# Head blocks of the memory update: eight narrow matmuls against two full ones with a mask

## The reference, cut to what matters

```
log_D = where(tril, cs[t] - cs[s], -inf) + ig[s];  D_mat = exp(log_D - max_log_D)
C = (q @ k.T / sqrt(32)) * D_mat                       # per head, 512 x 512
normalizer = max(|C.sum(-1)|, exp(-max_log_D))
h = (C / (normalizer + EPS)) @ v                       # then a layer norm over all heads
x = x + tanh(g_xattn) * h
```

## Time and profile before

| what | value |
| --- | --- |
| median of 3 runs | 799.27 us (798.9 to 800.16) |
| the profiled execution | 800.16 us, of which the span from first to last instruction is 798.2 us |
| busy, share of the span | PE 84%, DVE 64%, POOL 52%, ACT 47% |
| mean granted TensorE clock | 0.816 of 2.4 GHz |

### The profile page before, as it was taken

The page is one execution under the profiler, slowest core; times in us unless marked ns, Lnnn a source line. Parts: engine busy times, 40 slices in busy tenths (PEclk is TensorE's granted clock), DMA queues, the critical chain, the costliest instruction groups (busy, mean ns, idle before and its releaser), DMA issues.

```text
span 798.2 us, 18309 instructions
## 1 busy us (share of the span) xinstructions
PE 674.4 (84%) x6306; PEld 534.4 (67%) x6306; DVE 514.0 (64%) x1371; ACT 375.3 (47%) x941; POOL 411.3 (52%) x369
## 2 busy tenths in 40 slices
PE   2973879988998795067999999999999999999993
PEld 1531435554656564046998988989989889889893
DVE  7727787878877787973555564655555655555561
ACT  4335556766677754063444443443444443434441
POOL 5025499998998883012254444353444544534523
PEclk9995555555556655559999999999999999999998
DMA  9722878987988922173498897897988978969752
GB/s 285 263 94 61 246 249 270 292 244 255 302 273 271 290 105 67 14 303 122 133 276 271 241 286 232 236 307 217 272 261 261 273 245 236 309 206 287 252 147 50
DMA packets 85819, 179.74 MB, mean 225 GB/s; under 512 B 14881, under 2 KB 48546, under 8 KB 85730
## 3 DMA queue, kind: packets, MB, share of 16 engines
q1 hardware_dynamic: 63202, 140.10, 54.5%
q0 software_dynamic: 13824, 18.43, 10.9%
q10 hardware_dynamic: 8704, 20.06, 6.6%
HBM read 140.93 MB, written 38.67 MB: 225 GB/s over the span
## 4 chain that ended last, share of the span: by engine, by line
PE 51%; POOL 19%; DVE 11%; issue 9%; DMA 7%; ACT 2%; POOLq 0%; DVEq 0%; ACTq 0%
PE bank L1075 41%; POOL whl L469 8%; DMA out<-res,TS 4%; POOL x L699 3%; POOL vp L547 2%; DMA xg<-y_d,TG 2%; POOL qE L563 2%; PE bank L298 2%; PE bank L301 2%; PE bank L1069 2%; POOL kw L555 1%; POOL vp L545 1%; DMA w_d<-whl 1%; DVE R L970 1%; PE bank L510 1%
## 5 line engine op out<-in xcount | busy, mean ns | idle before, releaser
L1075 PE MATMUL bank<-xh,w 128*128 128x256 bf16 (+1 forms) x1760 | 268.2, 263 | 9.9 <-DVE xl L1131 8.2
L1057 POOL DMA_INDIRECT out<-res,TS x72 | 115.8, 1609 | 217.2 <-DMA out<-res,TS 97.8
L1075 PE MATMUL bank<-xl,w 128*128 128x256 bf16 (+1 forms) x880 | 222.5, 263 | 0.0
L1148 ACT ACTIVATE sg<-bank 128x256 f32<-128x256 f32 (+1 forms) x240 | 86.8, 362 | 232.2 <-PE bank L1075 220.1
L1075 PEld LDWEIGHTS bank<-xh,w 128*128 128x128 bf16 x1760 | 165.7, 98 | 28.5 <-issue 12.0
L1178 DVE TENSOR_TENSOR hf<-sg,bank 128x256 f32<-128x256 f32 (+1 forms) x200 | 78.9, 395 | 121.3 <-ACT sg L1148 114.7
L1075 PE MATMUL bank<-w,hh 128*128 128x256 bf16 x864 | 140.0, 273 | 0.0
L1048 POOL DMA_INDIRECT xg<-y_d,TG x72 | 72.5, 1006 | 79.0 <-DVE TS L1005 48.4
L469 POOL TENSOR_TENSOR whl<-wst,whl 128x1224 bf16<-128x1224 f32 x32 | 80.1, 2507 | 44.0 <-ACT whl L457 44.0
L1075 PE MATMUL bank<-w,hlo 128*128 128x256 bf16 x360 | 98.1, 273 | 0.0
L1142 ACT CAST hh<-hf 128x256 bf16<-128x256 f32 (+1 forms) x240 | 90.4, 377 | 12.6 <-DVE hf L1180 11.0
(11 more groups left out here) (218 smaller groups left out, 1079.9 us busy)
## 6 DMA issues: line engine op xcount, KB each, us to landing
w<-w_d SPq DMA_DIRECT2D x40, 1408.0 KB
w<-w_d SPq DMA_DIRECT2D x40, 768.0 KB
wst<-in_wts SPq DMA_DIRECT2D x32, 612.0 KB, 4.5
w_d<-whl ACTq DMA_DIRECT2D x32, 612.0 KB, 6.1
vb<-in_kv SPq DMA_DIRECT2D x8, 528.0 KB, 5.9
xa<-in_x SPq DMA_DIRECT2D x8, 512.0 KB, 8.3
kT<-in_kv SPq DMA_DIRECT2D x8, 512.0 KB, 8.8
xc<-in_x SPq DMA_DIRECT2D x8, 512.0 KB, 6.0
```

What stands on the lines that cost most here:

```text
L1057: nc.gpsimd.indirect_dma_start(out, bass.IndirectOffsetOnAxis(ap=TS[:, c0:c0 + 1], axis=0), res[w][:, j, :], None, bounds_check=TOK - 1, o ...
L1075: mm = nc.tensor.matmul(dst, l, r, start=(n == 0), stop=(n == len(pairs) - 1))
L1148: nc.scalar.activation(sg[m % 2][0:K, 0:N], bank[0:K, 2 + (NM * w + m) % 4, 0:N], ACT.Silu).then_inc(f_sg, 1)
```

## The change

The state update is computed as two full matmuls, all four heads of a group against all four; the blocks off the diagonal are then multiplied by zero on DVE, in the same operation that applies the scale 1/sqrt(32). For chunks 1 and 2 the masked product goes into a new SBUF tile `Ut`, and the update of the state reads `Ut` in place of PSUM. The mask `blkm` is made at the start, from one more index table on POOL and three more operations on DVE; the one clearing of PSUM goes away.

```diff
@@ consts_pool
+            nc.gpsimd.iota(blk[:, :].rearrange("p (h e) -> p h e", e=DV), [[DH, HG], [0, DV]], base=0,
+                           channel_multiplier=0, allow_small_or_imprecise_dtypes=True).then_inc(s_iota, 1)
@@ consts_dve
-            dve.wait_ge(s_iota, 4)
+            dve.wait_ge(s_iota, 5)
...
-
-            dve.wait_ge(s_const, 9)
+            nc.vector.tensor_scalar(blkt[:, :], blk[:, :], float(DH), pcol[:, 0:1], ALU.add, ALU.is_gt).then_inc(s_const, 1)
+            nc.vector.tensor_scalar(blkm[:, :], blk[:, :], pcol[:, 0:1], None, ALU.is_le).then_inc(s_const, 1)
+            dve.wait_ge(s_const, 11)
+            nc.vector.tensor_tensor(blkm[:, :], blkm[:, :], blkt[:, :], ALU.mult).then_inc(s_const, 1)
+
@@ g_actf_all
-                    nc.scalar.activation(dst, src, ACT.Copy, scale=SCALE).then_inc(g_cols, 1)
+                    nc.scalar.copy(dst, src).then_inc(g_cols, 1)
@@ g_pe_all, g_dvef
-            pe.wait_ge(b_uz, 1)
...
-            V.memset(bank[:, 4:6, UO:UO + HG * DV], 0.0).then_inc(b_uz, 1)
@@ b_s_pe
-                    for j in range(HG):
-                        hd = g * HG + j
-                        mm = nc.tensor.matmul(bank[DH * j:DH * (j + 1), 4 + g, UO + DV * j:UO + DV * (j + 1)],
-                                              kw[u % 2][:, DH * hd:DH * (hd + 1)], vv(u)[:, DV * hd:DV * (hd + 1)],
-                                              start=True, stop=True)
+                    mm = nc.tensor.matmul(bank[:, 4 + g, UO:UO + HG * DV], kw[u % 2][:, g * P:(g + 1) * P],
+                                          vv(u)[:, g * HG * DV:(g + 1) * HG * DV], start=True, stop=True)
@@ b_st_dve
-                ge(dve, b_h, t)
+                mask = blkm[:, :].unsqueeze(1).to_broadcast([P, 2, HG * DV])
                 if c == 0:
-                    V.tensor_copy(St[0][:, :, :], ub).then_inc(b_st, 1)
+                    ge(dve, b_h, t)
+                    V.scalar_tensor_tensor(St[0][:, :, :], ub, SCALE, mask, ALU.mult, ALU.mult).then_inc(b_st, 1)
                 else:
+                    V.scalar_tensor_tensor(Ut[:, :, :], ub, SCALE, mask, ALU.mult, ALU.mult).then_inc(b_ut, 1)
                     if t == 1:
                         ge(dve, s_dec, 16 * HG)
+                    ge(dve, b_ut, b * 2 + c)
+                    ge(dve, b_h, t)
                     for g in range(2):
                         ins = V.scalar_tensor_tensor(St[c % 2][:, g, :], St[1 - c % 2][:, g, :], dec[:, b, g, c:c + 1],
-                                                     ub[:, g, :], ALU.mult, ALU.add)
+                                                     Ut[:, g, :], ALU.mult, ALU.add)
```

More of the change, by code:

```diff
@@ L78, in build @@
         bank = ctx.enter_context(nc.psum_tensor("bank", [P, 8, 512], F32))
-        rowj = sb("rowj", [P, P]); rowjb = sb("rowjb", [P, P], BF16); pairj = sb("pairj", [P, HALF]); pcol = sb("pcol", [P, 1]);
+        rowj = sb("rowj", [P, P]); rowjb = sb("rowjb", [P, P], BF16); pairj = sb("pairj", [P, HALF]); pcol = sb("pcol", [P, 1]); blk = sb("blk", [P, HG * DV])
         tokp1 = sb("tokp1", [P, NT])
@@ L85, in build @@
         maskb = sb("maskb", [P, P], BF16); sel12 = sb("sel12", [12, HG])
-        selt = sb("selt", [12, HG]);
+        selt = sb("selt", [12, HG]); blkm = sb("blkm", [P, HG * DV]); blkt = sb("blkt", [P, HG * DV])
         eps_c = sb("eps_c", [P, 1]); neps_c = sb("neps_c", [P, 1]); revj = sb("revj", [P, NE]); one_c = sb("one_c", [P, 1])
@@ L113, in build @@
         kw = [attn(f"kw{w}", [P, D]) for w in range(2)]; St = [attn(f"St{w}", [P, 2, HG * DV]) for w in range(2)]
+        Ut = attn("Ut", [P, 2, HG * DV])
         n1 = attn("n1", [P, NH]); n2 = attn("n2", [P, NH]); n3 = attn("n3", [P, NH])
@@ L161, in build @@
         b_dl = sem("b_dl"); b_s = sem("b_s"); b_D = sem("b_D"); b_C = sem("b_C")
-        b_kw = sem("b_kw"); b_uz = sem("b_uz"); b_st = sem("b_st")
+        b_kw = sem("b_kw"); b_ut = sem("b_ut"); b_st = sem("b_st")
         b_h = sem("b_h"); b_n = sem("b_n"); b_ho = sem("b_ho")
@@ L206, in consts_pool @@
                 nc.gpsimd.memset(asb[w][:, :, :], 1.0).then_inc(s_mz, 1)
-        NCONST = 13
+        NCONST = 16
         def consts_dve(dve):
@@ L220, in consts_dve @@
             nc.vector.tensor_scalar(maskb[:, :], rowj[:, :], pcol[:, 0:1], NEG, ALU.is_lt, ALU.mult).then_inc(s_const, 1)
-            dve.wait_ge(s_const, 9)
+            nc.vector.tensor_scalar(blkt[:, :], blk[:, :], float(DH), pcol[:, 0:1], ALU.add, ALU.is_gt).then_inc(s_const, 1)
+            nc.vector.tensor_scalar(blkm[:, :], blk[:, :], pcol[:, 0:1], None, ALU.is_le).then_inc(s_const, 1)
+            dve.wait_ge(s_const, 11)
+            nc.vector.tensor_tensor(blkm[:, :], blkm[:, :], blkt[:, :], ALU.mult).then_inc(s_const, 1)
             nc.vector.tensor_tensor(selt[:, :], identf[0:12, 0:4], identf[0:12, 4:8], ALU.add).then_inc(s_const, 1)
-            dve.wait_ge(s_const, 10)
+            dve.wait_ge(s_const, 13)
             nc.vector.tensor_tensor(sel12[:, :], selt[:, :], identf[0:12, 8:12], ALU.add).then_inc(s_const, 1)
```

## The result

The changed kernel takes 819.46 us, median of 4 runs (819.11 to 820.06), beside 799.38 us (4 runs, 798.9 to 800.16) for the kernel before: a ratio of 1.0253, 95% interval 1.0239 to 1.0267. It is 20.1 us slower. The forecast was 821.3 us. The profiled execution of after took 819.85 us, its span 817.9.

A forecast was written before the change was run, and what follows sets the result against it. Bound taken: in the attention loop, a closed ring of POOL, PE, DVE and ACT, POOL and PE nearly full. Loop 20.9 plus constants 1.1 gives 22.0 us on 800.16, 822.2; against the 799.27 median 821.3 us, own range 813 to 828.

The forecast's parts named there:

- The lock: Attention loop: state updates with two SBUF inputs stand until POOL's L469 ends; 10.7 and 7.8 us for chunks 1 and 2; chance 0.68.
- locked slot: Loop slot updating chunk 1 or 2, where the state update stands behind L469; 1.68 to 0.8 us later in the worked examples.
- E: The end of POOL's L469 in a slot; L574 was to start at about E + 0.8, L699 at E + 4.44.
- The delays without the lock: Later matmul results and added mask work in the loop, 8.8 us, plus 1.1 us before it.
- The terms of the loop: Attention loop by slot kind: 10.7 (chunk 1) + 7.8 (chunk 2) + 3.9 (chunk 0) - 1.5 = 20.9 us.
- The weight stores: Loop slots waiting for a weight store have less traffic per microsecond to wait for; 1.5 us returned in all.
- The constants: Start of the kernel: new mask operations and revj stand behind POOL's clearings; +1.1 us, bounds 0.2 to 1.8.
- The experts: Expert steps, most of PE's share of the chain: not touched by the change, to last as long as before.
- Only the delays: Rival for the loop: L597 goes on inside L469, no lock; 8.8 us in the loop, 1.1 before, 809 us; chance 0.15.
- All is covered: Rival: PE and POOL idle enough and the weight stores decide; 800.5 us; chance 0.06.
- faster: Rival: full matmuls raise PE's granted clock from 1.2 to 2.4 GHz in the loop; 791.7 us; chance 0.03.
- Compounding: Rival: PE falls behind as well in the loop, 24 x 0.63 = 15 us on top; 834 us; chance 0.08.

The follow-up runs named there:

- e1: Changed kernel with the masked product written to PSUM instead of SBUF, so the state update has one SBUF input again: 804.98 us, ratio 1.0079.
- e2: Kernel before plus a copy of the update to SBUF for chunks 1 and 2, narrow matmuls, no mask: 814.99 us, ratio 1.0187.
- e5: Changed kernel with DVE's state update placed behind the masked scores, both SBUF inputs kept: 806.02 us, ratio 1.0097.
- e3: Kernel before with the wide matmuls alone, no mask, so part of the computation is left out: 802.03 us, ratio 1.0027.
- e4: Kernel before plus the new index table and three mask operations at the start, mask unused: 802.02 us, ratio 1.0027.
- e6: Kernel before with DVE's state update placed behind the masked scores: 800.23 us, ratio 1.0005.
- e10: Changed kernel with the state update behind the scores and POOL's clearings behind the constants: 801.14 us, ratio 1.0024.
- e7: Kernel before with POOL clearing mx and asb only once DVE has made its constants: 796.45 us, ratio 0.9979.
- e8: Kernel before with the state update behind the scores and POOL's clearings behind the constants: 795.64 us, ratio 0.9972.
- e9: Repeat of e8 with more rounds, same two edits on the kernel before: 797.2 us, ratio 0.9966.

## Why the prediction was right, and where its terms were off

- **The lock**, its main step, is shown from both sides: with everything else kept it goes with the operand (e1), and it comes with the operand and a copy alone (e2). With another order of DVE's work most of its cost goes too (e5). Its signs came as named: L602's median over 0.8 us, the gate's wait over 30, the loop's end at 330 (forecast 328). The rule of the Trainium skill ("SBUF — State Buffer", SBUF: two separate sides) that a DVE operation with two SBUF inputs and a GpSimd operation that reads SBUF exclude each other for the whole instruction is borne out by L602's 0.35 us turning into up to 2.65; L596, with one SBUF input and so outside the rule, stays at 0.43 in the same stretches.
- **Inside a locked slot** the steps came out nearly to the tenth. For E = 216.46: L575 at E + 0.70, L704 at E + 4.32 (forecast E + 0.8 and E + 4.44). For E = 225.08: E + 0.81 and E + 4.43 (forecast E + 4.54 for the gate). The 0.08 us from L664 to L699 isn't in the earlier trace rows, where the gate comes 0.37 us behind (206.30) because POOL is busy; a waiting gate of before has it (192.82 to 192.90), and the sum is right. The turns are as forecast, POOL's next operation between the two L602.
- **The size of the lock's term** was 821.3 - 809 = 12.3 us in the forecast and 14.5 by e1. One slot was missed: the prediction held that updates before 98 us stand behind nothing long. One stands at 96.66, behind the L473 of 96.62, and its first gate then waits 2.52 us:

```profile
96.62 2.50 POOL L473 TENSOR_TENSOR whl<-wst,whl 128x1224 bf16<-128x1224 f32 x1 [5.62 <-ACT whl L461]
...
103.55 0.72 POOL L704 TENSOR_TENSOR x<-x,lsg 128x256 f32<-128x256 f32 x1 [2.52 <-ACT x L669]
```

  Before, that L469 began at 93.27. Since all of the prologue moved, but not by the same amount on DVE and POOL, a list of locked slots taken from the rows of before was one short.
- **The delays without the lock** were put at 8.8 + 1.1 = 9.9 us; e1 gives 5.5 (4.2 to 8.3). Both parts were measured alone (e3, e4). What was too much is the 5.3 us for the slots with an update of chunk 1 or 2: in e1's trace the seven slots with chunk 0 grow by 5.1 us (3.5 forecast), and the twenty others shrink by 1.1 together. The operations themselves came close: 1.25 and 0.43 us for the 1.22 and 0.45 taken, 1.04 for 0.88 until PE's next line starts. Nothing is seen of a saving from one tiling change less.
- **The terms of the loop**, by the kind of slot, first to 28th gate of after less before: chunk 1 +6.4 us (forecast 10.7), chunk 2 +7.2 (7.8), chunk 0 +6.9 (3.9), and chunk 3, in which nothing was added, -3.0 (1.5 taken back over all slots). Another 2.8 us come before the first gate, where the missed slot lies, and 1.3 after the 28th. So the delay in the slots with chunk 0 came through in all seven of them, where the forecast halved it in the first four, and the slots with chunk 1 grew by 0.9 us and not by 1.3 to 1.7. The errors cancel: from the gates' end to the last gate the loop grew by 21.6 us, against 20.9 forecast. That the sum is this close is in part luck.
- **The weight stores** gave back more than the 1.5 us taken: ACT's wait for them fell by 14.7 us. The slots of chunk 3 are 3.0 us shorter together; how much of that is the stores' isn't separated.
- **The constants**: 1.29 us late, forecast 1.1, with revj behind the second clearing as forecast. The rest of the projections' 2.7 us isn't the change's: e2, e3 and e6, with constants ready at 10.32 as before, end them 1.05, 1.58 and 1.51 us later than the profiled execution of before. The first four projection matmuls (L298, 128x512 f32) took 2.40 us in that execution, 3.62 in e3, e6 and after, 3.45 in e2, and later groups of four take 1.88 in all of them. The granted clock reads 1.00 in all of these stretches, so the rise of the clock that the expectation of e4 names is not in that row; why the execution of before was quick there stays open.
- **The experts** were taken as equal, and are 4.1 us shorter in after with the same 4019 matmuls (start of the first gather to the end; columns as in the earlier trace rows). Before:

```profile
356.30:798.20 441.90, 415.82 (x4019) 372.58 (x4017) 242.59 (x672) 174.88 (x521) 188.25 (x144) 0.99 0.76 232
```

  and after:

```profile
380.10:817.90 437.80, 414.16 (x4019) 371.97 (x4017) 242.23 (x672) 174.23 (x521) 187.83 (x144) 0.99 0.76 234
```

  Only 1.7 us of it is PE's busy time, the rest is idle time that went. The single profiled executions of the other kernels give back between nothing and 4.2 us in the same stretch: e1, e3 and e10 about 4.1, e4 3.1, e5 2.7, e2 2.4, e6 and e7 about 1.1. And e8 and e9, which are one and the same kernel, give back 4.2 and 0.0. So this stretch varies by some 4 us from execution to execution, and the 4.1 us of after can't be told from that. By this, and not by a step of the loop, the prediction's 22.0 us met 19.7 in the span.
- **The rivals.** *Only the delays* (809) is the kernel that e1 makes, and was still 3 to 4 us too high. *All is covered* and *faster* are out with the ratio, the latter by the clock of 0.54. *Compounding* (834) is out as well: PE's own 24 x 0.66 us don't appear in the locked slots, since e2's locked slots are at least as long without them (8.46 and 8.72 us against 8.32 and 8.72).

## What to carry to other kernels

Before an operand of a DVE operation moves from PSUM to SBUF, count its SBUF inputs: with two, the operation stood here behind every long POOL operation reading SBUF that it met (up to 2.65 us for one of 0.35), and all that is queued behind it comes later too. If the tile must be in SBUF, put the operation behind the one that the slot waits for; that returned some 13 of 20 us with no arithmetic changed. A delay of PE or DVE in a ring that is only partly tight can cost a small share of count times delay (here 2.6 of 19 us, at most 4.1), because other slots give back what one loses. So time such a part alone before it is feared, and add up the slots by kind.

## What the runs showed of the hardware that was not expected

One clearing on POOL stops some DVE operations and lets others through. POOL's clearing of `mx` and DVE's constants in after:

```profile
6.93 3.64 POOL L208 MEMSET mx<- 24x4096 bf16 x1
10.53 1.02 POOL L209 MEMSET asb<- 24x1024 bf16 x1
```

```profile
6.21 0.93 DVE L224 TENSOR_SCALAR blkt<-blk,pcol 128x132 f32<-128x132 f32 x1
7.05 3.61 DVE L225 TENSOR_SCALAR blkm<-blk,pcol 128x132 f32<-128x132 f32 x1
10.70 0.29 DVE L227 TENSOR_TENSOR blkm<-blkm,blkt 128x132 f32<-128x132 f32 x1
11.18 0.40 DVE L234 TENSOR_SCALAR revj<-rowj 128x9 f32<-128x9 f32 x1
```

The tensor_scalar L225 stands until the clearing ends; the tensor_tensor L227, with two SBUF inputs, takes 0.29 us inside the next clearing, though in the loop an operation with two SBUF inputs stands behind L473. The rule of the Trainium skill ("SBUF — State Buffer", SBUF: two separate sides), read closely, has this: two SBUF inputs count only against a GpSimd operation that reads SBUF. By its row the clearing reads no tile, and L227 agrees, in this one case. revj, a tensor_scalar again, stands until 11.58, the end of that clearing (11.55), as forecast (11.4).

The loop before is irregular from slot to slot; with the lock it falls into a period of four slots that repeats to about 0.02 us. And the loop's length varies by some 3 us between single executions of kernels with the same loop: first to 28th gate 193.1 us in before, 194.7 in e7 and 196.6 in e4. That holds for the sums by kind of slot above as well. Of those sums only one kind repeats: the seven slots with chunk 0 are 4.2 to 6.9 us longer than in before in all five traces with wide matmuls (after, e1, e3, e5, e10), and within 1.2 us of it in all six with narrow ones. The parts of 2 to 3 us are therefore known from the repeated times, and not from a difference of two traces.
